# A decoder block's feed-forward phase: maxima searched a chunk behind, input turned earlier, weights split per group, first down chunk in pieces

## What is computed

```python
x = act_qdq(x)
up = act_qdq(x @ lpbq_dequant(w_up).T)
gate = act_qdq(x @ lpbq_dequant(w_gate).T)
sig = fixed_qdq_u16(jax.nn.sigmoid(gate))
gate = act_qdq(gate * sig)
o = act_qdq(gate * up)
return o @ lpbq_dequant(w_down).T
```

## Time and profile before

| | |
|---|---|
| median of 3 executions | 3137.54 us (3136.54 to 3139.95) |
| profiled execution: time, span | 3137.93 us, 3136.0 us |
| busy in the span: PE, DVE, ACT, POOL | 89%, 70%, 38%, 17% |
| mean granted TensorE clock | 0.947 of full |
| feed-forward phase | about 1278 to 3136 us of the span |

### The profile page before, as it was taken

The page is one execution under the profiler, slowest core; times in us unless marked ns, Lnnn a source line. Parts: engine busy times, 40 slices in busy tenths (PEclk is TensorE's granted clock), DMA queues, the critical chain, the costliest instruction groups (busy, mean ns, idle before and its releaser), DMA issues.

```text
span 3136.0 us, 33437 instructions
## 1 busy us (share of the span) xinstructions
PE 2783.9 (89%) x12272; PEld 2274.0 (73%) x12272; DVE 2191.6 (70%) x2213; ACT 1191.6 (38%) x1420; POOL 531.9 (17%) x311
## 2 busy tenths in 40 slices
PE   2589999999999998589999997799999958999998
PEld 2477777777877776477777775677777746888886
DVE  8668988988888988344444444688888876666654
ACT  2233444434344443233333334555555532222222
POOL 3111111121111111000000000111111114343431
PEclk7689999999999999799999998899999978999999
DMA  6212111111111111233333324556555653545543
GB/s 240 88 41 72 56 54 67 61 66 54 54 74 54 54 67 54 101 148 121 134 127 134 120 114 168 209 223 225 221 216 220 226 191 141 231 198 203 231 182 132
DMA packets 76559, 420.86 MB, mean 134 GB/s; under 512 B 8544, under 2 KB 8800, under 8 KB 36192
## 3 DMA queue, kind: packets, MB, share of 16 engines
q1 hardware_dynamic: 72912, 394.04, 32.9%
q10 hardware_dynamic: 3600, 26.22, 2.0%
HBM read 243.01 MB, written 177.21 MB: 134 GB/s over the span
## 4 chain that ended last, share of the span: by engine, by line
PE 46%; DVE 8%; issue 3%; ACT 2%; POOL 0%; DVEq 0%; POOLq 0%; ACTq 0%
PE ff_ps L1577 10%; PE ff_ps L1578 10%; PE ff_ps L1579 10%; PE ff_ps L1617 5%; PE ff_ps L1618 5%; PE ff_ps L1619 5%; DVE ff_lo L1341 2%; DVE ff_up_max L1372 1%; DVE ff_gs L1361 1%; DVE ff_prod L1375 1%; PE ff_ps L1568 1%; ACT ff_q L1188 1%; DVE ff_wl L1335 0%; ACT ff_group L1201 0%; DVE ff_cell_max L1377 0%
## 5 line engine op out<-in xcount | busy, mean ns | idle before, releaser
L1577 PE MATMUL ff_ps<-ff_hi,ff_wh 128*128 128x512 f32 x1536 | 622.7, 405 | 99.2 <-DVE ff_lo L1341 60.2
L1578 PE MATMUL ff_ps<-ff_lo,ff_wh 128*128 128x512 f32 x1536 | 615.3, 401 | 0.0
L1579 PE MATMUL ff_ps<-ff_hi,ff_wl 128*128 128x512 f32 x1536 | 613.8, 400 | 0.0
L1201 ACT ACTIVATE ff_group<-ff_ps,ff_scales 128x512 f32<-128x512 f32 x384 | 264.8, 690 | 683.2 <-PE ff_ps L1579 670.2
L1577 PEld LDWEIGHTS ff_ps<-ff_hi,ff_wh 128*128 128x128 f32 x1536 | 299.9, 195 | 170.2 <-issue 53.0
L1352 DVE TENSOR_REDUCE ff_gate_max<-ff_group 128x2048 f32 (+1 forms) x48 | 109.7, 2286 | 365.7 <-ACT ff_group L1201 365.7
L1579 PEld LDWEIGHTS ff_ps<-ff_hi,ff_wl 128*128 128x128 f32 x1536 | 298.9, 195 | 64.7
L1578 PEld LDWEIGHTS ff_ps<-ff_lo,ff_wh 128*128 128x128 f32 x1536 | 300.3, 195 | 62.1
L1617 PE MATMUL ff_ps<-ff_wh,ff_hi 128*128 128x512 f32 x768 | 299.9, 390 | 46.0 <-DVE ff_lo L1511 46.0
L1618 PE MATMUL ff_ps<-ff_wl,ff_hi 128*128 128x512 f32 x768 | 299.7, 390 | 0.0
L1619 PE MATMUL ff_ps<-ff_wh,ff_lo 128*128 128x512 f32 x768 | 299.5, 390 | 0.0
(11 more groups left out here) (193 smaller groups left out, 5356.4 us busy)
## 6 DMA issues: line engine op xcount, KB each, us to landing
gate_products<-ff_group SPq DMA_DIRECT2D x48, 1024.0 KB, 3.9
ff_raw<-gate_products SPq DMA_DIRECT2D x48, 1024.0 KB, 5.8
up_products<-ff_group SPq DMA_DIRECT2D x48, 1024.0 KB, 4.2
ff_raw<-up_products SPq DMA_DIRECT2D x48, 1024.0 KB, 9.3
gate_ints<-ff_gs SPq DMA_DIRECT2D x48, 512.0 KB, 2.6
ff_gs<-gate_ints SPq DMA_DIRECT2D x48, 512.0 KB, 9.9
xt_raw<-in_xT SPq DMA_DIRECT2D x64, 256.0 KB, 2.8
csq<-in_ctx_rows SPq DMA_DIRECT2D x16, 1024.0 KB, 6.5
```

The lines of the kernel that those rows point to most:

```text
L1201: act.activation(group[:, g, m * T:(m + 1) * T], out_ps[(GM * g + m) % 6][:], ACT.Copy, scale=s_x).then_inc(evacuated, 1)
L1577: pe.matmul(o, wh[:, m, k], hi[:, par, k], start=(k == 0), stop=False)
L1578: pe.matmul(o, wh[:, m, k], lo[:, par, k], start=False, stop=False)
L1579: mm = pe.matmul(o, wl[:, m, k], hi[:, par, k], start=False, stop=(k == KC - 1))
```

## The change

- The input of the next block is turned after output tiles 3 and 5 of a gate step; ACT quantizes transposes 0 and 1 after the first chunk's evacuations, and 2 and 3 in the middle of the second chunk's; DVE's `low` comes ahead of the second chunk's reductions. The first block is turned into four banks at once.
- Weights: groups 0 and 1 are split before the scale of the input is formed, group 2 right behind `quantize`. The three groups of up are split in the last gate step, each behind its chunk on ACT and DVE. SP's order around the stage change stays: `load_weights(5)` comes behind the three `load_gate`. Load 8 is issued in the last up step.
- Search: ACT forms |up| of a chunk (`magnitude`, one more 128 x 2048 pass), DVE does product and maximum in one instruction per cell of 512 (`tensor_tensor_reduce`, four a chunk) and a small copy, one chunk behind, after L1372 of that chunk and `gated` of the next. It takes signed products with |up|; the check is widened for the small negative ones. The last chunk is done in quarters. `high` comes after the first chunk of an up step, `low` ahead of the second.
- After the search: the two cells are loaded before the decision is known, DVE (not POOL) rounds up chunks 0 and 1, and the first down chunk goes through product, `hi`, `lo` and PE in four pieces of 128 rows.

The diff, cut to what the steps speak of:

```diff
+                        if not ahead and g == 1:
+                            load_weights(2 * NG + 2)
...
                 load_x2(1, 1)
-                store_q(0, 0)
                 load_weights(2)
                 load_weights(3)
+                store_q(0, 0)
                 load_weights(4)
...
-                load_weights(8)
...
+                sp.wait_ge(cells_known, 1)
+                places = [sp.value_load(best_at[0:1, n:n + 1], min_val=0, max_val=NCH * GM - 1) for n in range(QUICK)]
+                for n in range(QUICK):
+                    chunk = nc.s_assert_within(places[n] >> 2, 0, NCH - 1, skip_runtime_bounds_check_because=(
+                        "a cell below NCH * GM shifted by two is below NCH"))
+                    cols = bass.ds((places[n] & 3) * T, T)
+                    sp.dma_start(cand_up[:, n], up_dram[chunk, :, cols]).then_inc(cand_in, 16)
+                    sp.dma_start(cand_g[:, n], gs_chunks[chunk, :, cols]).then_inc(cand_in, 16)
                 every = all_needed(sp)
...
-                pool.wait_ge(packed_ready, 2)
+                pool.wait_ge(packed_ready, 1)
+                pool.wait_ge(cell_ready, NCH)
...
-                    if not (first and g < 2):
-                        pool.wait_ge(o16_ready, t - 1)
-                    pool.wait_ge(tick_done, NCH + t)
+                    pool.wait_ge(o16_ready, t + TT - 2)
+                    pool.wait_ge(tick_done, NCH + t - 2)
...
-                round_up(0, 0, 0, True)
-                round_up(0, 0, 1, True)
-                round_up(0, 0, 2, True)
+                pool.wait_ge(up16_ready, 2)
+                round_up(0, 0, 2)
...
+                def quantize(b, par, tiles, turn_to=turn_ps):
+                    for c in tiles:
...
-                        evacuate(b, par, g, range(GM))
-                        if first and g < NG - 1:
-                            weights_high(g + 1)
+                        evacuate(b, par, g, (0, 1))
                         if g == 1 and ahead:
-                            quantize(b + 1, 1 - par)
+                            quantize(b + 1, 1 - par, (2, 3))
+                        evacuate(b, par, g, (2, 3))
+                        if g == 0 and ahead:
+                            quantize(b + 1, 1 - par, (0, 1))
+                        if not ahead:
+                            weights_high(NG + g)
...
+                def magnitude(t, par, g, cols=slice(0, CH)):
+                    act.activation(up_abs[:, (NG * par + g) % 2, cols], group[:, g, cols], ACT.Abs).then_inc(abs_ready, 1)
...
+                            act.wait_ge(up_max_ready, t - 2)
+                        if g == NG - 1 and not ahead:
+                            act.wait_ge(search_ready, GM * (t - 1))
+                            for m in range(GM):
+                                evacuate(NB + b, par, g, (m,))
+                                act.wait_ge(evacuated, GM * (NG * (NB + b) + g) + m + 1)
+                                magnitude(t, par, g, slice(m * T, (m + 1) * T))
+                        else:
+                            evacuate(NB + b, par, g, (0, 1))
                             gate_chunk_16(nb, npar, ng, first and ng > 0)
-                        evacuate(NB + b, par, g, (2,))
-                        if more:
+                            evacuate(NB + b, par, g, (2,))
                             gate_chunk_sigmoid(nb, npar, ng)
-                        evacuate(NB + b, par, g, (3,))
-                        if first and g < NG - 1:
-                            weights_high(NG + g + 1)
+                            evacuate(NB + b, par, g, (3,))
+                            act.wait_ge(evacuated, GM * (NG * (NB + b) + g + 1))
+                            wait(act, search_ready, GM * (t - 1))
+                            magnitude(t, par, g)
+                        if g == 0 and ahead:
+                            high(b + 1, 1 - par)
                         if not ahead:
                             weights_high(2 * NG + g)
-                        if g == 1 and ahead:
-                            high(b + 1, 1 - par)
...
                 weights_high(0)
+                weights_high(1)
                 act.wait_ge(scale_ready, 2)
-                quantize(0, 0)
+                quantize(0, 0, range(KC), banks[0:KC])
+                weights_high(2)
                 gate_step(0, 0, True, True)
...
-                act.wait_ge(stored[0], 16 * (NB - 1))
-                act.wait_ge(gate_max_ready, 2 * (NG * (NB - 2)) + 2)
-                evacuate(NB - 1, 1, 0, range(GM))
-                weights_high(NG)
-                act.wait_ge(stored[1], 16 * (NB - 1))
-                act.wait_ge(gate_max_ready, 2 * (NG * (NB - 2) + 1) + 2)
-                evacuate(NB - 1, 1, 1, range(GM))
+                gate_step(NB - 1, 1, False)
                 high(0, 0)
-                act.wait_ge(stored[2], 16 * (NB - 1))
-                act.wait_ge(gate_max_ready, 2 * (NG * (NB - 2) + 2) + 2)
-                evacuate(NB - 1, 1, 2, range(GM))
                 act.wait_ge(top_ready, 1)
...
+                def oh_first():
+                    for j in range(TT):
+                        rows = slice(j * P, (j + 1) * P)
+                        act.wait_ge(o16_ready, j + 1)
+                        act.activation(hi[:, 0, :, rows], o16[:, 0].bitcast(I16).rearrange("p (k t) -> p k t", t=T)[:, :, rows],
+                                       ACT.Copy).then_inc(oh_ready, 1)
+
...
-                        if g == 2 and ahead:
+                        if g == 1 and ahead:
                             low(b + 1, 1 - par)
-                        if first and g > 0:
-                            weights_low(g)
+                        if first and g == 0:
+                            weights_low(2)
-
-                def gated(b, par, g):
+                        if not ahead:
+                            weights_low(NG + g)
...
+                    if after is not None:
+                        dve.wait_ge(abs_ready, after + 1)
+                        dve.wait_ge(gs_ready, after + 1)
+                        wait(dve, cell_ready, after - 1)
                     dve.scalar_tensor_tensor(gs16[:, g], sr16[:, sl], gs_factor, g16[:, sl], ALU.mult, ALU.mult).then_inc(gs_ready, 1)
 
+                def search(par, g, m):
+                    sl = (NG * par + g) % 2
+                    cols = slice(m * T, (m + 1) * T)
+                    dve.tensor_tensor_reduce(up_abs[:, sl, cols], gs16[:, g, cols], up_abs[:, sl, cols], 1.0, -3e38, ALU.mult, ALU.max,
+                                             cells[:, sl, m:m + 1]).then_inc(search_ready, 1)
+
+                def keep_cells(t, par, g):
+                    dve.wait_ge(search_ready, GM * (t + 1))
+                    dve.tensor_copy(cell_max[:, bass.ds(GM * t, GM)], cells[:, (NG * par + g) % 2]).then_inc(cell_ready, 1)
+
                 def up_step(b, par, ahead, first=False):
+
                     for g in range(NG):
                         t = NG * b + g
-                        nb, npar, ng = (b, par, g + 1) if g < NG - 1 else (b + 1, 1 - par, 0)
-                        if g == 2 and ahead:
+                        if g == 1 and ahead:
                             low(NB + b + 1, 1 - par)
-                        if first and g > 0:
-                            weights_low(NG + g)
-                        dve.wait_ge(evacuated, GM * (NG * (NB + b) + g + 1))
-                        dve.tensor_reduce(up_max[:, bass.ds(t, 1)], group[:, g], AX.X, ALU.max,
+                        pb, ppar, pg = (b, par, g - 1) if g > 0 else (b - 1, 1 - par, NG - 1)
+                        if first and g == 0:
+                            gated(b, par, g)
+                            continue
+                        dve.wait_ge(evacuated, GM * (NG * (NB + pb) + pg + 1))
+                        dve.tensor_reduce(up_max[:, bass.ds(t - 1, 1)], group[:, pg], AX.X, ALU.max,
                                           apply_absolute_value=True).then_inc(up_max_ready, 1)
-                        dve.tensor_tensor(prod[:, 0], gs16[:, g], group[:, g], ALU.mult).then_inc(prod_ready, 1)
-                        dve.wait_ge(prod_ready, t + 1)
-                        dve.tensor_reduce(cell_max[:, bass.ds(GM * t, GM)], prod[:, 0].rearrange("p (m t) -> p m t", t=T), AX.X,
-                                          ALU.max, apply_absolute_value=True).then_inc(cell_ready, 1)
-                        if g < NG - 1 or ahead:
-                            gated(nb, npar, ng)
-                        if not ahead and g < NG - 1:
-                            weights_low(2 * NG + g)
-
+                        gated(b, par, g, t - 1)
+                        for m in range(GM):
+                            search(ppar, pg, m)
+                        keep_cells(t - 1, ppar, pg)
+                        if not ahead and g > 0:
+                            weights_low(2 * NG + g - 1)
+
```

(49 more changed lines are left out.)

93 lines of the change are left out of this document (49 added, 44 removed).

## The result

| | before | after |
|---|---|---|
| median of 4 executions each, same chip | 3137.70 us | 2964.28 us (2962.84 to 2966.83) |
| ratio of the times | | 0.9447, 95% interval 0.9431 to 0.9464 |
| span of the profiled execution | 3136.0 us | 2963.0 us |
| busy: PE, DVE, ACT, POOL | 89%, 70%, 38%, 17% | 92%, 72%, 43%, 17% |
| mean granted TensorE clock | 0.947 | 0.965 |

The forecast was 2963.

The account below looks back on a forecast made before the run. PE's chain from 1295 us to the end was taken as the bound. Terms 17.9 + 43.3 - 13.8 + 31.1 + 75.6 + 20.7 = 174.8 us, taken from 3137.93, gave 2963 us, range 2946 to 3000.

Parts of the forecast that it names:

- The path: PE's chain from 1295 us to the end; each edit is worth the PE wait and slow clock it removes.
- Start and stage change: Start with gate step 0: gain 17.9 us; gate to up: loss 13.8 us, PE waiting on load 5's chain.
- The lower bound of 5 us: Smallest loss allowed between gate and up, if load 5 lands like the fastest of its kind.
- Gate steps: Gate steps 1 to 14: no wait for `quantize`, 34.42 us each instead of 37.51, gain 43.3 us.
- Up steps: Up steps 1 to 14: no wait for `lo`, 32.64 us each instead of 38.04, gain 75.6 us.
- The search's price: DVE in the up stage: 0.7 us assumed per search instruction, 12 a step, DVE's step 26.2 us.
- Rival 1: Up stage and tail: search at half rate, 1.3 us more each, DVE bounds the stage; 2983 us, chance 15%.
- rival 2: Up stage: ACT pays two table loads a chunk, 35.1 us a step; 3000 us, chance 5%.
- rival 3: Gate stage keeps its wait for `quantize`, nothing of the 43.3 us comes; 3006 us, chance 10%.
- Rival 4: Up stage: search runs like the scan, 2.35 us, DVE's step 46.0 us; slower, 3177 us, chance 3%.
- Tail: From ACT's last evacuation to PE's start of down: E + 24.6 instead of E + 45.3, gain 20.7 us.
- the next late thing: Down's start: POOL rounds chunk 2, then chunk 1's `lo` by E + 36.9; PE needs it at E + 37.9.

Follow-up runs that it names:

- (6): Changed kernel with one spare reduction of 128x2048 per up chunk on DVE, result unused: 2971.28 us.
- (8): Changed kernel with load 5 issued in the last gate step, behind the store of its second chunk, not behind the three gate reads: 2950.29 us.
- (2): Changed kernel with turns after tiles 5 and 7 and `low` ahead of the third chunk, as before; only ACT's `quantize` kept split: 2963.29 us.
- (4): Kernel before with only two up-stage moves: `high` behind a step's first chunk, `low` ahead of the second; old search: 3061.48 us.
- (5): Changed kernel with the up stage's `high` behind the second chunk and `low` ahead of the third, as before; new search kept: 2966.13 us.
- (3): Changed kernel with the search of all chunks but the last in two instructions, product and reduction, still a chunk behind: 2967.28 us.
- (1): Changed kernel with the gate stage's old order: turns after tiles 5 and 7, `quantize` in one go, `low` ahead of the third chunk: 3009.78 us.
- (7): Changed kernel with two spare reductions of 128x2048 per up chunk on DVE, results unused: 3053.85 us.
- 9: Changed kernel with chunks 0 and 1 of down rounded up by POOL again instead of DVE: 2972.31 us.
- 10: Changed kernel with the first down chunk's product, `hi` and `lo` in one piece instead of four: 2966.24 us.
- (11): Changed kernel with load 5 earlier, first up step's `high` and `low` in the last gate step, start reordered, DVE rounding chunk 2: 2932.50 us.

## Why the prediction was right, point by point

**The path.** That only PE's waits, with the slower clock behind them, count is borne out from both sides: the waits went and the span fell by 173 us, and loading DVE to 37.45 of 38 us (6) cost nothing within the stage.

**Start and stage change.** 18.1 against 17.9, -13.7 against -13.8. The loss was put down to load 5 and the chain behind it, and (8) gives it back: 14.0. It landed after 11.0 us where the forecast had kept the landing of before (9.5 us, issued 1.4 earlier), which comes to the same within 0.1. The lower bound of 5 us for it (a load like the fastest) wasn't near.

**Gate steps.** 34.46 against 34.42 a step. The forecast named ACT's start of `quantize` as the cause, and (2) shows it to be all of it. Where the transposes stand, which its text gives equal room, is not what pays.

**Up steps.** 32.65 a step against 32.64. The cause named, `lo` behind a whole chunk's search, holds. The forecast took the move of `high` and `low` as what places `lo` early, and the search only as a load that mustn't exceed PE's time. (4) bears out just that. What it didn't see is that the new search would have done alone (5), and that two instructions in its place, a chunk behind, cost 2.5 us and those in the tail (3). So the fused instruction buys DVE 4.8 us of slack a step (358.5 busy against 426.1 over the same 14 steps) and little else, since DVE isn't the bound.

**The search's price.** 0.7 taken, 0.69 measured undisturbed, 0.82 in the mean. Rival 1 (half rate, 1.3) falls. The Trainium skill's Vector Engine (DVE) Microarchitecture Reference, Points that are easy to get wrong, has the half rate for a scalar-tensor-tensor form with two non-bf16 sources in SBUF; neither L1388 (2.34 us for 2048 columns) nor the search (0.69 for 512, as long as a reduction of 512, 0.68) shows it. DVE's up step, put at 26.2, is 25.6 and ACT's, put at 27.4, is 27.3. That DVE's comes so near is in part luck: with their mean of 0.82 the 12 searches cost 1.4 more than at 0.7, and the rest of the sum came out 2.0 smaller.

**The other rivals.** There is one table load in the up stage, so rival 2 falls. No row for `quantize`, so rival 3 falls; (1) gives its price, 45.5 where it was put at 43.3. Rival 4's bound of DVE above 32.64 us is real, shown by (7), at a load that the search never came near.

**Tail.** +21.1 against +20.7. POOL's rounding (9, 10.9 us at PE's start) and the pieces (10, 4.7) carry it on the chip. The rest, the last chunk in quarters and the cells loaded before the decision, has no run of its own. Inside the chain the 0.4 is partly luck. The index of the cells was there at E + 5.6, not 7.0, but from it to the rounding of the candidates it took 10.3 us, where the forecast had 8.3; POOL's reduction took 1.4 us and not 2.4.

**What was missed.** The sum was 1.8 us too large, of which 1.5 is the down stage, put at nothing; 1.2 of these are one wait. The text had named chunk 2's rounding on POOL as the next late thing, with 1 us of margin. It was eaten:

```profile
2427.72 2.35 DVE L1561 SCALAR_TENSOR_TENSOR ff_sr<-ff_gs,ff_scales,ff_g 128x2048 int16<-128x2048 int16 x1
2432.95 4.17 DVE L1561 SCALAR_TENSOR_TENSOR ff_sr<-ff_gs,ff_scales,ff_g 128x2048 int16<-128x2048 int16 x1 [2.88 <-POOL ff_g L1160]
2437.04 2.28 DVE L1583 TENSOR_TENSOR ff_lo<-ff_sr,ff_hi 128x2048 fp32r<-128x2048 int16 x1
```

```profile
2439.37 0.50 PE L1694 MATMUL ff_ps<-ff_wh,ff_hi 128*128 128x512 f32 x1 [1.20 <-DVE ff_lo L1583]
```

POOL's rounding was done at E + 32.4, near the forecast (32.2). But the product behind it took 4.17 us instead of 2.35, while POOL's next rounding ran beside it (below), so `lo` of chunk 1 came 2.0 us later and PE waited 1.20. The step that failed is "product and the `lo` of chunk 1 behind it by E + 36.9": it was E + 38.9. In (11), where DVE rounds chunk 2, the wait is gone.

## What to carry to other kernels

Before pricing a new instruction, ask which wait the change removes and which of its edits is enough alone: here two pairs of edits went with one wait each, and in each pair one edit was enough; a move of two lines in the kernel before gave 76 us, as much as both edits of the up stage together. An engine that is busy for 98% of a stage cost nothing in it, since nobody waited for its last result, and 7 us once the stage was over; look instead for what stands ahead of the result that is waited for. When a wait is moved, follow every queue it passes: one DMA left behind three others cost 14 us, and the rest of that chain, until it was laid beside PE's work, another 13.
